# 32x32 transposes on VectorE instead of 128x128 transposes on TensorE in the second layer

## The reference

```
x = x + ffn0(cond0(x))      # cond0: a mixed 128x128 matrix per batch; ffn0: W (2048x2048) and 16 low-rank updates
x = x + ffn1(conv1(x))
conv1: grouped convolution (4 groups of 32 channels, 9 taps, pad 4) + context + bias
ffn1:  t = conv1(x).reshape(4096, 2048)[:, perm].reshape(4096, 16, 128)
       t = einsum('bhd,hdm->bhm', t, up)      # 128 -> 512 per head
       t = gelu(t, exact)
       t = einsum('bhm,hmd->bhd', t, down)    # 512 -> 128 per head
       t.reshape(4096, 2048)[:, argsort(perm)]
```

## Time and profile before

| | us |
|---|---|
| median of three executions | 2582.73 |
| the profiled execution | 2583.87 |
| its span | 2582.0 |
| TensorE busy | 2528.0 |
| VectorE busy | 1822.8 |
| ScalarE busy | 1001.8 |
| GpSimd busy | 950.8 |

### The profile page before, as it was taken

How to read it: one execution, slowest core, us unless ns; L and a number is a source line. 1 busy time by engine, 2 the same in 40 slices (tenths; PEclk the granted TensorE clock), 3 DMA queues, 4 the chain that set the end, 5 groups by cost and what they waited for, 6 DMA issues and landing times.

```text
span 2582.0 us, 39106 instructions
## 1 busy us (share of the span) xinstructions
PE 2528.0 (98%) x12090; PEld 2099.3 (81%) x12090; DVE 1822.8 (71%) x2667; ACT 1001.8 (39%) x1632; POOL 950.8 (37%) x826
## 2 busy tenths in 40 slices
PE   8899999999999999999999999999999999999997
PEld 6788888888888888888888778888888888888775
DVE  6665555965556755576445768888888888888876
ACT  3221212321122322232222555555555555555573
POOL 2366645466654455233223212222222222222231
PEclk9999999999999999999999999999999999999998
DMA  9965644665545777576555754577767676777786
GB/s 318 322 196 199 201 168 155 238 210 197 196 163 185 228 229 228 161 250 210 160 165 186 223 153 131 170 219 219 221 214 226 205 223 205 225 226 223 212 281 240
DMA packets 417281, 541.02 MB, mean 210 GB/s; under 512 B 36248, under 2 KB 270064, under 8 KB 417072
## 3 DMA queue, kind: packets, MB, share of 16 engines
q1 hardware_dynamic: 314816, 307.40, 39.6%
q10 hardware_dynamic: 78144, 154.27, 15.9%
q0 software_dynamic: 24112, 76.80, 9.4%
HBM read 309.72 MB, written 228.61 MB: 208 GB/s over the span
## 4 chain that ended last, share of the span: by engine, by line
PE 91%; DVE 4%; DMA 2%; issue 2%; ACT 1%; ACTq 0%; SPq 0%; POOL 0%; DVEq 0%; POOLq 0%
PE ps_c L461 44%; PE ps_up L1398 13%; PE ps_y L1408 13%; PE ps_c L1423 9%; PE ps_v L439 4%; PE ps_c L427 2%; PE ps_zt L1436 2%; PE ps_f L1444 2%; DVE w_lo L1004 1%; PE ps_up L1423 1%; DVE ring_lo L951 0%; DVE r_early L1000 0%; DMA a_s<-in_lora_a 0%; DMA x_n<-in_up 0%; DMA aggw_d<-agg 0%
## 5 line engine op out<-in xcount | busy, mean ns | idle before, releaser
L461 PE MATMUL ps_c<-w_hi,ring_hi 128*128 128x512 f32 x1792 | 703.8, 393 | 3.8 <-DVE r_early L1000 3.2
L461 PE MATMUL ps_c<-w_hi,ring_lo 128*128 128x512 f32 x1792 | 698.0, 390 | 0.0
L461 PE MATMUL ps_c<-w_lo,ring_hi 128*128 128x512 f32 x1792 | 697.8, 389 | 0.0
L611 ACT ACTIVATE ring_hi<-raw_n 128x512 fp32r<-128x512 f32 x382 | 239.4, 631 | 848.7 <-DVE raw_n L942 235.1
L1380 POOL DMA_INDIRECT y_d<-y_s,idx x128 | 145.7, 1139 | 723.1 <-ACT y_s L1548 689.6
L1505 ACT ACTIVATE kern<-ps_up 128x512 f32<-128x512 f32 x512 | 306.6, 599 | 257.5 <-PE ps_up L1398 245.4
L461 PEld LDWEIGHTS ps_c<-w_hi,ring_hi 128*128 128x128 f32 x1792 | 336.7, 188 | 74.5 <-issue 4.0
L461 PEld LDWEIGHTS ps_c<-w_hi,ring_lo 128*128 128x128 f32 x1792 | 336.4, 188 | 70.2
L461 PEld LDWEIGHTS ps_c<-w_lo,ring_hi 128*128 128x128 f32 x1792 | 336.7, 188 | 67.3
L1622 DVE TENSOR_TENSOR g_lo<-kern,g_hi 128x512 fp32r<-128x512 f32 x512 | 354.5, 692 | 38.2 <-ACT g_hi L1509 21.8
L1000 DVE TENSOR_TENSOR r_early<-ps_c,r_early 128x512 f32<-128x512 f32 x256 | 176.6, 690 | 276.2 <-PE ps_c L461 276.2
(11 more groups left out here) (211 smaller groups left out, 3832.9 us busy)
## 6 DMA issues: line engine op xcount, KB each, us to landing
u_d<-raw_n ACTq DMA_DIRECT2D x64, 512.0 KB, 3.2
x_d<-r_early ACTq DMA_DIRECT2D x128, 256.0 KB, 3.6
raw_n<-u_d SPq DMA_DIRECT2D x64, 512.0 KB, 3.6
x_d<-x_s ACTq DMA_DIRECT2D x126, 256.0 KB, 2.7
u_s<-x_d SPq DMA_DIRECT2D x496, 64.0 KB, 2.2
z_d<-x_s SPq DMA_DIRECT2D x120, 256.0 KB
rear<-y_d SPq DMA_DIRECT2D x112, 256.0 KB
rear<-x_d SPq DMA_DIRECT2D x112, 256.0 KB, 4.0
```

The source lines that it names most:

```text
L461: mm = nc.tensor.matmul(bank, a[:, dc, :], w[k][:, dc, :], start=(first and dc == 0 and n == 0), stop=(dc == 3 and n == 2), skip_group_che ...
L611: nc.scalar.activation(ring_hi[g % RING][:].rearrange("p a n -> p (a n)"), factor(q, k, p), ACT.Copy).then_inc(hi_ready, 1)
```

## The change

Both turns leave TensorE. VectorE's transpose turns each 32x32 square of a 128x512 tile in place of its partition group; to make that enough, the data is laid out so that squares are all that has to be turned. Units of the convolution go by channel group first (batch 0 to 3 of group 0, then group 1): the tile for z then holds 32 channels of 4 batches, with position 4(32w + i) + r at partition 32r + i, and the z store is one DMA for each r on 32 partitions. The final units go by phase: y is loaded as four DMAs on 32 partitions, turned by VectorE into `results`, and x1 of the same phase is added in place without a stride. The output is stored by phase (the host reorders it), in 512-byte pieces. VectorE's `turn_z` takes the place of the copy; it waits for z itself, and ScalarE's next z waits for it. In all steps ScalarE now casts chunks 0 and 2 of g, VectorE 1 and 3. After the last step TensorE still turns y by 64 transposes, in another order; the adds are without a stride, and the output goes in 64 DMAs of 64 KB, half from SP and half from ScalarE.

```diff
-        yt_s = [rear[:, j, :].rearrange("p (l r) -> p l r", l=4) for j in range(2)]
-        x1_s = [rear[:, 2 + j, :].rearrange("p (s q) -> p s q", s=S) for j in range(2)]
+        yt_s = [rear[:, j, :] for j in range(2)]
+        x1_s = [rear[:, 2 + j, :] for j in range(2)]
...
-        zt_pair = [sh.x1_s[:].rearrange("p a (w s c) -> p (a w) s c", w=2, s=S),
-                   rear[:].rearrange("p w (s c) -> p w s c", s=S)]
+        zt_pair = [flat.rearrange("p (w b c) -> p w b c", w=WIDE, b=SB)
+                   for flat in (sh.x1_s[:].rearrange("p a n -> p (a n)"), rear[:].rearrange("p w n -> p (w n)"))]
...
-        def by_scalar(k, h, mc):
-
-            return late(k, h) and mc % 2 == 1
-
-        def scalar_copies(k, h, mc):
-            return 2 * (H * k + h - (STEPS - LEAD + 1)) + mc // 2 + 1
+        def by_scalar(mc):
+
+            return mc % 2 == 0
+
+        def cast_count(k, h, mc):
+
+            return MC // 2 * (H * k + h) + mc // 2 + 1
...
         def conv_unit(k, h):
 
-            return H * k + h + LEAD, h % 2, SB * k + (h + LEAD) // G, h % G
+            group, batch = divmod((h + LEAD) % H, SB)
+            return H * k + h + LEAD, h % 2, SB * k + SB * ((h + LEAD) // H) + batch, group
 
         def final_unit(k, h):
 
-            return H * (k - 1) + h, h % 2, SB * (k - 1) + h // 4, h % 4
+            return H * (k - 1) + h, h % 2, h // 4, h % 4
+
+        def final_part(dram, k, phase, q):
+
+            first = SB * (k - 1)
+            return dram[bass.ds(first, SB), :, phase, q * P:(q + 1) * P].rearrange("b c q -> c b q")
+
+        def z_rows(dram, r, part):
+
+            return dram.rearrange("(w i r) n -> r i w n", w=WIDE, r=S)[r, :, :, part * C:(part + 1) * C]
...
-                sp.dma_start(yt_s[j], y_d[1 - parity][c * 512:(c + 1) * 512, h // 4 * C:(h // 4 + 1) * C]
-                             .rearrange("(l p) r -> p l r", p=P)).then_inc(yt_in[j], 16)
+                rows = y_d[1 - parity].rearrange("(q w i s) n -> q s i w n", q=4, w=4, s=S)[q, phase]
+                for g in range(G):
+                    sp.dma_start(yt_s[j][g * GC:(g + 1) * GC, :].rearrange("p (w n) -> p w n", w=4),
+                                 rows[:, :, g * C:(g + 1) * C]).then_inc(yt_in[j], 16)
                 wait(sp, o_ready, v - 1)
-                sp.dma_start(x1_s[j], x1_d[b, :, :, c * P:(c + 1) * P]).then_inc(x1_in[j], 16)
+                sp.dma_start(x1_s[j].rearrange("p (b q) -> p b q", b=SB),
+                             final_part(x1_d, k, phase, q)).then_inc(x1_in[j], 16)
...
                 for c in range(4):
-                    sp.dma_start(last_yt[c], y_d[(BLOCKS - 1) % 2][c * 512:(c + 1) * 512, :]
-                                 .rearrange("(l p) r -> p l r", p=P)).then_inc(last_yt_in[c], 16)
+                    sp.dma_start(last_yt[c], y_d[(BLOCKS - 1) % 2].rearrange("(l p s) r -> s p l r", l=4, s=S)[c]).then_inc(last_yt_in[c], 16)
...
-                sp.dma_start(out[b, :, c * 512:(c + 1) * 512], o_s[j]).then_inc(o_out[j], 16)
+                sp.dma_start(final_part(out, k, phase, q), o_s[j].rearrange("p (b q) -> p b q", b=SB)).then_inc(o_out[j], 16)
...
-                for w in range(2 if isinstance(u, int) and u == H - 1 else 4):
-                    sp.dma_start(z_d[(parity + ahead) % 2][w * 512:(w + 1) * 512, jb * C:(jb + 1) * C]
-                                 .rearrange("(q r) n -> q r n", r=S), zt_of(*before(k, h, 2))[:, w, :, :]).then_inc(z_out[jb % 2], 16)
+                for r in range(2 if isinstance(u, int) and u == H - 1 else S):
+                    sp.dma_start(z_rows(z_d[(parity + ahead) % 2], r, jb),
+                                 zt_of(*before(k, h, 2))[r * GC:(r + 1) * GC].rearrange("p w b c -> p w (b c)")).then_inc(z_out[jb % 2], 16)
...
             drive(sp, step)
             finish()
+            for v in range(H):
+                store_last(sp, v, range(2))
...
-            def turn_z(k, h):
-                u, _, _, _ = conv_unit(k, h)
-                z = z_pair[pair_of(k, h)]
-                if isinstance(k, int) and u == 0:
-                    pe.wait_ge(small_in, 32)
-                    pe.wait_ge(sh.u_read[1], 4 * QUADS)
-                pe.wait_ge(z_ready, u + 1)
-                wait(pe, zt_ready, u)
-                for w in range(4):
-                    mm = nc.tensor.transpose(ps_zt[:, 0, w * P:(w + 1) * P], z[:, w * P:(w + 1) * P], id_s[:])
-                mm.then_inc(zt_done, 1)
-
-            def turn_y(k, h):
-                v, j, _, _ = final_unit(k, h)
-                pe.wait_ge(yt_in[j], 16 * (H // 2 * (k - 1) + h // 2 + 1))
-                wait(pe, o_ready, v)
-                for l in range(4):
-                    mm = nc.tensor.transpose(ps_f[:, 0, l * P:(l + 1) * P], yt_s[j][:, l, :], id_s[:])
-                mm.then_inc(fin_done, 1)
-
             def step(k, h, parity):
                 if exists(k, h, LEAD):
                     conv(k, h)
-                if exists(k, h, LEAD - 1):
-                    turn_z(*before(k, h))
-                if final_exists(k, h, 1):
-                    turn_y(*before(k, h))
...
                 for l in range(4):
-                    mm = nc.tensor.transpose(last_ps[v % 4][:, l * P:(l + 1) * P], last_yt[c][:, l, b * C:(b + 1) * C], id_s[:])
+                    mm = nc.tensor.transpose(last_ps[v % 4][:, l * P:(l + 1) * P], last_yt[c][:, l, g * C:(g + 1) * C], id_s[:])
...
-                if by_scalar(k, h, mc):
+                if by_scalar(mc):
                     act.wait_ge(gelu_done, MC * s + mc + 1)
-                    act.wait_ge(down_done, MC * (s - 1) + mc + 1)
+                    wait(act, down_done, MC * (s - 1) + mc + 1)
                     nc.scalar.activation(g_hi[:, mc, :], g_s[:, mc, :], ACT.Copy).then_inc(ghi_scalar, 1)
...
                     act.wait_ge(conv_done, u + 1)
-                    wait(act, zt_done, u - 1 if paired(k, h) else u)
+                    wait(act, zt_ready, u - 1 if paired(k, h) else u)
...
             for v in range(H):
-                b, c = last_unit(v)
-                act.wait_ge(last_o, v + 1)
-                act.dma_start(out[b, :, c * 512:(c + 1) * 512], last_sum[v]).then_inc(last_o_out, 16)
-            act.wait_ge(last_o_out, 16 * H)
+                store_last(act, v, range(2, SB))
+            act.wait_ge(last_o_out, 64 * H)
...
-            def take_z(k, h):
-                u, j, b, g = conv_unit(k, h)
-                dve.wait_ge(zt_done, u + 1)
+            def turn_z(k, h):
+                u, _, b, _ = conv_unit(k, h)
+                dve.wait_ge(z_ready, u + 1)
                 if isinstance(k, int) and u == 0:
                     for p in range(2):
                         for blk in range(4):
                             dve.wait_ge(sh.r_out[p][blk], 16 * QUADS)
-                if g == 0:
-                    q = (h + LEAD) // G
-                    if isinstance(b, int) and b <= SB:
-                        wait(dve, z_out[q % 2], 64 * (b // 2))
+                part, n = divmod(h + LEAD, SB)
+                if n == 0:
+                    tile = SB * k + part
+                    if isinstance(tile, int) and tile <= SB:
+                        wait(dve, z_out[part % 2], 64 * (tile // 2))
                     else:
-                        wait(dve, z_out[(q + 1) % 2], 64 * (SB // 2 * k + (q + 1) // 2))
-                nc.vector.tensor_copy(zt_of(k, h)[:, :, :, g * GC:(g + 1) * GC],
-                                      ps_zt[:, 0, :].rearrange("p (w r o) -> p w r o", w=4, r=S)).then_inc(zt_ready, 1)
-
-            def take_final(k, h):
-                v, j, b, c = final_unit(k, h)
+                        wait(dve, z_out[(part + 1) % 2], 64 * (SB // 2 * k + (part + 1) // 2))
+                nc.vector.transpose(zt_of(k, h)[:, :, n % SB, :], z_pair[pair_of(k, h)]
+                                    .rearrange("p (w c) -> p w c", w=WIDE)).then_inc(zt_ready, 1)
+
+            def turn_y(k, h):
+                v, j, _, _ = final_unit(k, h)
+                n = H // 2 * (k - 1) + h // 2
+                dve.wait_ge(yt_in[j], 64 * (n + 1))
+                wait(dve, o_out[j], 16 * n)
+                nc.vector.transpose(o_s[j].rearrange("p (b w i) -> p b w i", b=SB, w=4),
+                                    yt_s[j].rearrange("p (w b c) -> p b w c", w=4, b=SB)).then_inc(fin_done, 1)
...
+            def add_x1(k, h):
+                v, j, _, _ = final_unit(k, h)
                 n = H // 2 * (k - 1) + h // 2
                 dve.wait_ge(fin_done, v + 1)
                 dve.wait_ge(x1_in[j], 16 * (n + 1))
-                wait(dve, o_out[j], 16 * n)
-                nc.vector.tensor_tensor(o_s[j].rearrange("p (q s) -> p q s", s=S),
-                                        ps_f[:, 0, :].rearrange("p (q s) -> p q s", s=S),
-                                        x1_s[j].rearrange("p s q -> p q s"), ALU.add).then_inc(o_ready, 1)
```

(25 more changed lines are left out.)

45 lines of the change are left out of this document (26 added, 19 removed).

## The result

The changed kernel takes 2617.7 us (median of 4 runs, 2617.3 to 2623.0) against 2582.4 (4 runs): ratio 1.0136, 95% interval [1.0115, 1.0158]. It is 1.4% slower, clear of the noise; the forecast was 2553 us and faster. The profiled execution took 2622.95 us with a span of 2621.1, 39.1 more than the span of before.

The account below looks back on a forecast made before the run. TensorE bounded the kernel; after the change a ring of VectorE and ScalarE would. Full steps -15.5, first block -6.5, late -8.2, lead -3.3, block starts +6, end -2.4: -29.9 us, to 2553 us, range 2500 to 2625.

Parts of the forecast that it names:

- rival (a): VectorE's transposes are slow, so the ring is longer than TensorE's old step: slower, 2629 us at T = 1.085; chance 0.24.
- The ring: Full steps: VectorE and ScalarE wait on one another in a loop of 6.86 + 2T, 8.26 us, against 8.43 before; -15.5 us.
- T: Time of one VectorE transpose, taken as 0.70 us; the change was to lose above 0.85.
- I take 1 us for each of 6 blocks, +6 (bounds 0 and 2 us each): Block starts: SyncE waits for the last scatter, has more issues to catch up, and turn_y of the second unit comes late.
- The store ... 0: The z store in 512-byte pieces waits nowhere near its use, so it costs 0.
- The late steps, -8.2: Last 19 steps, without convolution or z: no ring, 5.75 us a step against 6.18, as g_lo waits for ScalarE's casts.
- The first block, -6.5: First 17 steps, with turn_z alone: the ring without turn_y is 7.64 us, -0.38 a step.
- The lead, -3.3: The lead's units: TensorE needs 0.35 us less each, but SP's issues at 0.59 let only half be gained.
- The end, -2.4: The 16 final adds lose their stride, 4.8 us at most; half taken, since y and output still move then.
- (b): TensorE stays the bound because the ring is shorter than thought: whole gain of -112 us, 2471 us; chance 0.12.
- (c): SP's queue becomes the bound: eleven issues at 0.86 us make a step of 9.5, 2657 us; chance 0.06.

Follow-up runs that it names:

- h1: The changed kernel with its z store over 128 partitions a DMA, as before the change, rows of z_d out of order; 2591.0 us.
- h3: The changed kernel with h1's z store and the y load as one DMA over 128 partitions (that load alone: 2596.8 us); 2577.3 us.
- e2: The changed kernel, but VectorE turns z before it turns y; 2601.5 us.
- e7: The changed kernel, but after the lead VectorE turns z in its own step, behind xp_lo, and z is stored one step earlier; 2607.6 us.
- e3: The changed kernel, but in the late steps ScalarE casts chunks 1 and 3 instead of 0 and 2; 2610.2 us.

## Why the prediction was wrong

The measured 2617.7 lies inside the stated 2500 to 2625 only because that range reached out for rival (a), slow transposes, and they were not slow. By stages the sum was off by 68 us (-29.9 against +38.5); 28 of them are the block starts, 21 the late steps.

- **The ring.** Mechanism and T right: z late by 2.7 us, up waits for t_lo, 8.18 against 8.26. This gave 0.25 us on 90 steps, 22 us, and 3 in the first block: the only gains there were.
- **"I take 1 us for each of 6 blocks, +6 (bounds 0 and 2 us each)"** is the step that failed first. The six starts cost 33.5 us over a step of 8.15, about 5.6 each (one of them in the first 17 steps). The prediction named SyncE's catching up, but priced it at turn_y, and of the z store it said "waits nowhere near its use, 0". In the trace of before, the copy of z already waited 1.0 to 1.3 us at five of the six starts: the slack was nothing, so 1.9 us of y issues, 0.9 of z issues and 2.1 of landing went almost whole into VectorE's wait and from there into TensorE's time (h1 to h3).
- **"The store ... 0"** failed in the other steps too: each fourth step between the block starts loses up to 1.4 us to it, 8.8 in all. A faster step makes this worse: in e2 and e7 the excess grows by 17.
- **The late steps, -8.2.** They became +12.8. The term counted VectorE's load and let g_lo wait for casts. That the cast of chunk 2 stands on ScalarE ahead of t_hi and y_s, with TensorE's next down behind, was in the order of instructions and wasn't priced: 0.6 us a step. Nor was the gain there: with the casts back in their places the step is 6.20, as before the change (e3).
- **The first block, -6.5.** Step 16 aside it is 7.82, not 7.64, so 3 us of the gain are missing. The prediction had the ring alone there; the second chain, through up, the Gelu and cast of chunk 2 and y_s, is 7.8 and sets the step.
- **The lead, -3.3.** It became +6.6. The issue price of 0.59 was taken where no z store was near; in the lead a z store costs up to 0.92 an issue, and the queue is full. Part of the +6.6 is noise: leads with untouched code differ by 4 us. The end, -2.4, became +1.2; not tried.
- **The rivals.** (a) fell with T = 0.70, (b) with the 8.18. (c) had the right place, SyncE, and the wrong form: not eleven issues at 0.86 a step (they fit into it) but a queue that is late once a block. Its sentence on 32-partition transfers, which reach 8 of 16 ports (the Trainium skill, "SBUF — State Buffer", "Door 1: The DMA port swizzle"), pointed to what mattered, and was set aside because the x1 loads had been such transfers before. The runs agree with it as far as the landing of the z store got longer, 5.3 us against 4.2 (h1); they don't show ports.

## What to carry over

A transfer's slack is read at its worst place, not in the ordinary step: find where its wait already shows, even 1 us in five places, and take anything added ahead of it in that queue at full price. When one link leaves a ring, look for the next chain before the gain is booked: here it was 0.35 us shorter than the ring. When a result moves from PSUM to a tile in SBUF that a store reads, it takes on that store's wait. If several transfers are wanted behind one wait, their order only chooses the one that is late; here a second buffer gave 15 us, reordering 7, and the buffer with one reordering 37.

## What the runs showed of the hardware

- VectorE's transpose of 128x512 in fp32, in 32x32 blocks, takes 0.685 (turn_z) to 0.705 us (turn_y), and starts follow one another by 0.62. The add of a PSUM and an SBUF tile of the same size took 1.085 with a stride of 4 in its operands, and 0.68 to 0.69 without one (the last 16 adds of the changed kernel).
- The same bytes in the same 512-byte pieces cost SyncE 0.92 us an issue when the SBUF side was 32 partitions and 0.68 when it was 128 (3.69 and 2.72 for four, in the lead; 1.0 and 0.8 at a block's start). The order of the rows in DRAM differed too.
